# Two-segment ScalarE and VectorE instructions, and a new deal of the PSUM banks, in a two-layer similarity kernel

## The reference

```python
s = box_sum(box_sum(x, 1, 1), 2, 5)               # width sum
num = box_sum(s * s, 3, 20)                       # channel sum
d = box_sum(box_sum(box_sum(x * x, 1, 1), 2, 5), 3, 20)
return jnp.nan_to_num(num / (d * norm), nan=1.0)  # norm: columns inside the window
```

## Time and profile before

| | |
|---|---|
| time, median of 3 runs | 6088.27 us (6087.27 to 6088.81) |
| profiled execution, first to last instruction | 6085.2 us |
| TensorE matmul busy | 5723.6 us, 94% |
| ScalarE busy | 5014.0 us, 82% |
| VectorE busy | 4144.7 us, 68% |
| GpSimd busy | 3546.7 us, 58% |
| mean granted TensorE clock | 0.998 of full speed |
| store of a tile, from issue to landing, median | 18.1 us (18.2 in the first layer) |

### The profile page before, as it was taken

How to read it: one execution, slowest core, us unless ns; L and a number is a source line. 1 busy time by engine, 2 the same in 40 slices (tenths; PEclk the granted TensorE clock), 3 DMA queues, 4 the chain that set the end, 5 groups by cost and what they waited for, 6 DMA issues and landing times.

```text
span 6085.2 us, 139173 instructions
## 1 busy us (share of the span) xinstructions
PE 5723.6 (94%) x49196; PEld 5710.7 (94%) x49196; DVE 4144.7 (68%) x9033; ACT 5014.0 (82%) x8201; POOL 3546.7 (58%) x1043
## 2 busy tenths in 40 slices
PE   0089999999999999999999999999999999999999
PEld 0089999999999999999999999999999999999999
DVE  9988889988877766767667555555555555555555
ACT  0078888888888888888888888888888888888888
POOL 0056665566556666666665666666666666666665
PEclk9999999999999999999999999999999999999999
DMA  9946655556633433434334344343434434343343
GB/s 367 367 157 212 223 207 191 207 203 215 220 125 125 151 138 134 156 124 153 137 135 147 132 147 143 129 160 124 159 130 141 149 124 165 124 153 137 135 154 124
DMA packets 660641, 1007.81 MB, mean 166 GB/s; under 512 B 5168, under 2 KB 660528, under 8 KB 660528
## 3 DMA queue, kind: packets, MB, share of 16 engines
q1 hardware_dynamic: 660528, 1006.65, 47.1%
HBM read 603.98 MB, written 402.65 MB: 165 GB/s over the span
## 4 chain that ended last, share of the span: by engine, by line
PE 89%; DVE 8%; issue 2%; ACT 1%; DMA 0%; SPq 0%; DVEq 0%; POOL 0%; POOLq 0%; ACTq 0%
PE width_ps L468 43%; PE den_ps L492 23%; PE num_ps L492 23%; DVE out_stats L555 3%; DVE lane_mv L562 2%; DVE y_out L649 1%; DVE newton L631 1%; DVE recip L637 0%; DMA y_out<-in_x_dram 0%; DVE beside_stats L555 0%; ACT recip L398 0%; ACT recip L401 0%; SPq L198 0%; DVEq L555 0%; PE num_ps L443 0%
## 5 line engine op out<-in xcount | busy, mean ns | idle before, releaser
L312 POOL TENSOR_TENSOR centred<-x_in,mean_row 128x1536 f32<-128x1536 f32 x512 | 1771.0, 3459 | 1415.0 <-PE width_ps L468 1097.5
L321 POOL TENSOR_TENSOR y_out<-x_in,y_out 128x1536 f32<-128x1536 f32 x512 | 1771.4, 3460 | 1117.1 <-DVE y_out L649 1117.1
L631 DVE SCALAR_TENSOR_TENSOR newton<-den_ps,recip 128x384 f32<-128x384 f32 x2048 | 1110.7, 553 | 1884.7 <-ACT recip L401 1854.8
L492 PE MATMUL den_ps<-band_c,tT 128*128 128x138 f32 (+2 forms) x12288 | 1809.0, 283 | 9.6 <-DVE newton L631 9.6
L492 PE MATMUL num_ps<-band_c,sT 128*128 128x138 f32 (+2 forms) x12288 | 1732.6, 284 | 20.4 <-DVE recip L637 20.1
L468 PE MATMUL width_ps<-band_w,centred 128*128 128x130 f32 x12288 | 1628.3, 275 | 0.5 <-DVE rvar_col L620 0.5
L468 PE MATMUL width_ps<-band_wc,square 128*128 128x130 f32 x12288 | 1625.5, 275 | 0.0
L492 PEld LDWEIGHTS den_ps<-band_c,tT 128*128 128x128 f32 x12288 | 1608.9, 190 | 13.3 <-DVE newton L631 11.8
L492 PEld LDWEIGHTS num_ps<-band_c,sT 128*128 128x128 f32 x12288 | 1580.5, 190 | 27.7 <-DVE recip L637 22.9
L388 ACT ACTIVATE sT<-width_ps,rstd_col 128x512 f32<-128x512 f32 x1536 | 1035.8, 674 | 592.9 <-PE width_ps L468 592.9
L468 PEld LDWEIGHTS width_ps<-band_w,centred 128*128 128x128 f32 x12288 | 1507.0, 191 | 0.9 <-DVE rvar_col L620 0.9
(11 more groups left out here) (44 smaller groups left out, 302.8 us busy)
## 6 DMA issues: line engine op xcount, KB each, us to landing
x_in<-in_x_dram SPq DMA_DIRECT2D x80, 3072.0 KB, 11.0
first_layer_out<-y_out SPq DMA_DIRECT2D x64, 3072.0 KB, 18.2
x_in<-first_layer_out SPq DMA_DIRECT2D x64, 3072.0 KB, 10.9
out_dram<-y_out SPq DMA_DIRECT2D x63, 3072.0 KB, 18.1
beside<-in_x_dram SPq DMA_DIRECT2D x30, 3072.0 KB, 11.0
y_out<-in_x_dram SPq DMA_DIRECT2D x18, 3072.0 KB, 24.4
out_dram<-y_out SPq DMA_DIRECT2D x4, 768.0 KB, 3.5
```

Source lines behind the costliest of these rows:

```text
L312: nc.gpsimd.tensor_tensor(centred[e % 2][:], x_in[slot][:, g * PSEG:(g + 1) * PSEG, :], mean_row[ph % 2][:].unsqueeze(1).to_broadcast([P, ...
L321: nc.gpsimd.tensor_tensor(y_out[slot][:, g * PSEG:(g + 1) * PSEG, :], x_in[slot][:, g * PSEG:(g + 1) * PSEG, :], y_out[slot][:, g * PSEG:( ...
L492: last = nc.tensor.matmul(bank[:, lo:hi], data[:, k, at:at + P], band_c[k][:], start=(k == 0), stop=(k == KB - 1), skip_group_check=True)
L631: nc.vector.scalar_tensor_tensor(newton[:, i, :], den_ps[i % 3][:, 0:C], TINY, recip[par][:, i, :], ALU.add, ALU.mult).then_inc(den_used, 1)
```

## The change

The three parts of the PSUM deal and the widening go together.

- ScalarE: `squares` is one instruction of 1536 instead of two of 768. `invert` works on two segments at once (768 elements out of two banks): 2 Ln and 2 Exp a pair instead of 4 and 4. Its step is S0 T0 L0 S1 T1 Q S2 T2 L1.
- VectorE: `approach` and `weigh` work on two segments at once, 2 and 2 a pair instead of 4 and 4. The result of `approach` goes into `y_out`, where it will be divided in place; the buffer `newton` is gone. The waits for the store of the tile before and for its measurement move from `divide` to the first `approach`. The step is approach 0, weigh 0, approach 1, weigh 1, divide; the three parts of `measure_beside` stand behind approach 0, weigh 0 and approach 1.
- PSUM: `width_ps` is 2 banks, one for S and one for T. `den_ps` is two double banks, D0 and D1 in one, D2 and D3 in the other. `num_ps` is one double bank for N0 and N1 and then for N2 and N3.
- TensorE: N1 is moved ahead of S2 and D2 behind it. The done counts go up once for two segments.
- At a change of phase, the request for the group mean stands behind the last `weigh`, where it was ahead of it.

```diff
-        newton = sb("newton", [P, PSEG, C])
...
-        width_ps = [... for i in range(3)]   # [P, 2 * W]
-        den_ps = [... for i in range(3)]     # [P, 512]
-        num_ps = [... for i in range(2)]     # [P, 512]
+        width_ps = [... for i in range(2)]   # [P, 2 * W]
+        den_ps = [... for i in range(2)]     # [P, 2, 512]
+        num_ps = ...                         # [P, 2, 512]
...
+                    nc.scalar.activation(square[par][:], centred[par][:], ACT.Square).then_inc(rows_squared, 1)
...
-                    src = width_ps[u % 3][:]
+                    src = width_ps[is_t][:]
...
+                    both = recip[par][:, 2 * h:2 * h + 2, :]
+                    nc.scalar.activation(both, den_ps[h][:, :, 0:C], ACT.Ln, bias=bias_ln[:],
+                                         scale=LN_SCALE).then_inc(log_done, 1)
+                    act.wait_ge(log_done, (base + p) * 2 + h + 1)
+                    nc.scalar.activation(both, both, ACT.Exp, bias=bias_exp[:], scale=-1.0).then_inc(recip_done, 1)
...
-                    for what in ("S0", "L0", "T0", "L1", "S1", "Q0", "T1", "L2", "Q1", "S2", "T2", "L3"):
+                    for what in ("S0", "T0", "L0", "S1", "T1", "Q", "S2", "T2", "L1"):
...
-                    if not (is_opening(ph, p, 1) and u < 3):
+                    if not (is_opening(ph, p, 1) and u < 2):
-                        pe.wait_ge(width_taken, (ph * NPAIR + p) * UNITS + u - 2)
+                        pe.wait_ge(width_taken, (ph * NPAIR + p) * UNITS + u - 1)
...
+                        bank, data = num_ps[:, i % 2, :], sT[par]
+                        if i % 2 == 0 and not (is_opening(ph, p, 1) and h == 0):
+                            pe.wait_ge(num_used, pair * 2 + h)
...
+                        bank, data = den_ps[h][:, i % 2, :], tT[par]
+                        if i % 2 == 0 and not is_opening(ph, p, 1):
+                            pe.wait_ge(den_used, pair * 2 + h - 1)
...
-"S0", "F1", "D0", "F2", "T0", "D1", "S1", "F3", "N0", "T1", "D2", "S2", "N1", "T2", "D3", "N2", "N3"
+"S0", "F1", "D0", "F2", "T0", "D1", "S1", "F3", "N0", "T1", "N1", "S2", "D2", "T2", "D3", "N2", "N3"
...
+                    nc.vector.scalar_tensor_tensor(y_out[slot][:, at:at + 2, :], den_ps[h][:, :, 0:C], TINY,
+                                                   recip[par][:, 2 * h:2 * h + 2, :], ALU.add, ALU.mult
+                                                   ).then_inc(den_used, 1)
...
+                            approach(ph, p, par, 0, i, lo, e)
+                            measure_beside(ph, i, lo, e, 0)
                             weigh(ph, p, par, 0)
+                            measure_beside(ph, i, lo, e, 1)
+                            approach(ph, p, par, 1, i, lo, e)
+                            measure_beside(ph, i, lo, e, 2)
                             weigh(ph, p, par, 1)
```

More of the change, by code:

```diff
@@ L360, in finish_logs, with squares @@
                                          scale=-0.5).then_inc(log_given, 1)
[L362 to L370, removed]
+                def squares(ph, p, par):
+                    act.wait_ge(rows_centred, ph * NPAIR + p + 1)
+                    if not is_opening(ph, p, 2):
+                        act.wait_ge(width_done, (ph * NPAIR + p - 1) * UNITS)
+                    nc.scalar.activation(square[par][:], centred[par][:], ACT.Square).then_inc(rows_squared, 1)
                 def take(ph, p, par, k, is_t):
@@ L411, in step @@
                         elif what[0] == "Q":
                             if ph2 < NP_:
-                                squares(ph2, p2, par, n)
+                                squares(ph2, p2, par)
                         elif ph1 < NP_:
-                            take(ph1, p1, 1 - par, n, int(what[0] == "T"))
+                            take(ph1, p1, 1 - par, int(what[1]), int(what[0] == "T"))
                 finish_logs(0)
                 for p in range(2):
-                    for half in range(2):
-                        squares(0, p, p, half)
+                    squares(0, p, p)
@@ L442, in finish_part @@
                         for half in range(2):
-                            last = nc.tensor.matmul(num_ps[part - 1][:, 0:GROUPS], over_p[:],
+                            last = nc.tensor.matmul(num_ps[:, part - 1, 0:GROUPS], over_p[:],
                                                     stat_two[:, 2 * (part - 1), half, :],
@@ L447, in finish_part @@
                         for k in range(KB):
-                            last = nc.tensor.transpose(den_ps[2][:, P * k:P * (k + 1)],
+                            last = nc.tensor.transpose(den_ps[1][:, 0, P * k:P * (k + 1)],
                                                        rstd_row[:, P * k:P * (k + 1)], identity[:])
@@ L623, in finish @@
                     dve.wait_ge(params_ready, ph + 1)
-                def approach(ph, p, par, i):
-                    dve.wait_ge(recip_done, (ph * NPAIR + p) * PSEG + i + 1)
-                    if i == 0 and not is_opening(ph, p, 1):
-                        dve.wait_ge(ratio_done, ph * NPAIR + p)
-                    nc.vector.scalar_tensor_tensor(newton[:, i, :], den_ps[i % 3][:, 0:C], TINY,
-                                                   recip[par][:, i, :], ALU.add, ALU.mult).then_inc(den_used, 1)
```

90 lines of the change are left out of this document (38 added, 52 removed).

## The result

The changed kernel takes 6131.37 us (6131.34 to 6133.99, 4 runs) against 6087.77 (6086.86 to 6088.81, 4 runs) of the kernel before on the same chip: 1.0073 times as long, 95% interval 1.0058 to 1.0087. That is slower, as forecast, but by 43.6 us where 17.4 were forecast, and 1.4 us above the range.

A forecast was written before the change was run, and what follows sets the result against it. TensorE, busy 94% of the span, was taken as the bound, with 56.5 us lost to win. Terms 16 + 2 - 4 + 2.4 + 1 = +17.4 us on 6085.2, plus 3.1 for the median, gave 6106; range 6092 to 6130.

The forecast's parts named there:

- Edit 2: In measured tiles N2 waits for weigh 0 behind a longer chain: 0.59 us a tile, 27 tiles, +16 us.
- Edit 1: ScalarE's fewer, wider instructions: gain nothing; the take of S1 ends 0.5 us before S2 needs its bank.
- Edit 3: Stretches of totals, where VectorE sets the pace: +2 us for three in the first phase, -4 for three later.
- Edits 4: Change of phase: TensorE's first F part waits 1.2 us more for VectorE's request; two outside the totals, +2.4 us.
- 5: The tail: last Ln and Exp 0.6 us longer, `approach` and `weigh` 0.8 between them, some overlapped before: +1 us.
- 6: Waits moved to the first `approach`: stores land well before the next `approach` into their buffer, so nothing.
- A: Rival: the waits of N2 for weigh 0 in measured tiles don't appear; 6090, no change; chance 0.20.
- B: Rival: faster, the chain also fits the stretches of totals and waits for `den_ps` go; -12 us, 6076; chance 0.06.
- C: Rival: wide ScalarE instructions cost two narrow ones, S2 waits in each pair; 6180 to 6230; 0.06 with other cliffs.
- D: Rival: granted clock falls more often after longer or denser waits; +6 us, 6112; counted within the forecast's 0.68.

The follow-up runs named there:

- experiment 1: Changed kernel with the first part of the measuring beside placed behind weigh 0 instead of ahead of it: 6101.92 us, ratio 1.0024.
- experiment 7: Kernel before with two width banks, one for S and one for T, in place of three in turn: 6088.48 us, ratio 1.0001.
- Experiment 2: Changed kernel with two single numerator banks and a narrow `weigh`, four times a pair over one segment: 6119.02 us, ratio 1.0051.
- experiment 3: Changed kernel with a narrow `invert`: Ln and Exp over one segment each, four of each a pair: 6107.22 us, ratio 1.0033.
- experiment 5: Changed kernel with `weigh`, numerator banks, Ln and Exp all narrow; `approach` stays wide over double denominator banks: 6095.67 us, ratio 1.0013.
- number 9: Kernel before with five of its six stretches of totals spread, each set over seven pairs, mostly 4 groups a pair: 6075.82 us, ratio 0.9981.
- 6: Changed kernel with `weigh`, numerator banks, Ln, Exp narrow, first measuring part behind the second `weigh`, mean request ahead of the last: 6092.49 us, ratio 1.0007.
- 4: Changed kernel with the buffer `newton` back and the waits for the store and the measurement back at `divide`: 6126.19 us, ratio 1.0062.

## Why the prediction came out as it did

**Edit 2 was right, in mechanism and in size.** Predicted were 0.23 + 0.10 and 0.16 + 0.10 us in a measured tile, 0.59 together. Measured: steps that are 0.38 and 0.26 us longer than 11.117, 0.64 together, the waits being 0.28 and 0.16. D3 to N2 took 12.12 and 12.38 us where the sum said 12.07 (4 groups) and 12.33. The order of the terms held too: with the first part of the measuring moved, experiment 1, the loss is nil.

**Edit 1 was right.** The stated cover of 0.5 us holds for all 510 pairs; no wait of a width unit for a take appears, with the wide Ln and Exp or, in experiment 7, without them. In a late pair the take of S1 ends at 5549.77 and S2 starts at 5550.35, a cover of 0.58. I took 0.30 us more for 384 more elements. Measured are 901 - 578 = 323 ns for Ln and 936 ns less the 0.61 us of the earlier trace rows for Exp: 0.84 and 0.85 ns an element. That agrees with the 0.833 of the Trainium skill (ScalarE: Activation LUTs, What happens when an `exp` ACTIVATE runs) better than with my 0.77.

**Edit 3 is the step that failed.** For a later stretch the prediction put "three more pairs cost 3 x 0.87 + 0.98 + 1.67 + 2.09 + 3.8 - 11.12 = 0.0 to 0.1 and a restart each: 2.8 against 4.1". It added up VectorE's work and took it for the period, as if VectorE never waited while it is the slowest. It does wait, about 1 us in each pair of the first later stretch: 0.93 for N2 and N3 in the first turn, since one double bank serves both of its `weigh`, and 1.14, 0.93 and 1.14 for ScalarE's Exp in the others. The prediction charged the chain from D3 to N2 once a stretch, where every D3 that is on time starts it anew. So the last three pairs there lost 1.12, 1.33 and 1.12 us where it had 0.0 to 0.1 and a restart, and N2 waited four times a stretch and not once. Measured are 6.0, 7.7 and 7.7 us, together 13 us more than forecast; 9.7 of these are the mechanism and 3.3 the clock. Experiment 2 took the exchange away, 3 shortened the chain, 5 did both, and these gave back 0.8, 0.6 and 1.5 us of the 1.9 that a stretch costs more than before, with the clock left out. In the first phase the stretches cost 7 us more than the +2 forecast; how those divide between chain, exchange and the clock (below) no run here separates, but experiment 5 gives 6.2 us back there and experiment 1, with less in the chain, 7.8.

**Terms that weren't in the sum at all:** 5.1 us at the starts of loop bodies and 1.1 in the first body, where 16 groups stand behind a `divide` in place of 8. **Edits 4, 5 and 6** came out at 2.0 for 2.4, 1.4 for 1, and no wait for a store. As forecast, TensorE loses nothing more once the last change of phase (3361 to 3373 us) is over.

**The rivals.** A (no waits) fell: they are there, at the predicted place. B (faster, as the waits ahead of the denominators go) had half of its mechanism: those waits are gone, but the totals made the numerators late instead. The rule of the Trainium skill on few large instructions (VectorE: DVE Perf Modes, The TRN2 errata) agrees in direction with VectorE's row: 2048 instructions fewer took 167 us off its busy time, 0.08 us each. The kernel became slower all the same. C (twice the price) fell with 936 ns where it needed 1220. D (the clock) came true, and may have cost more than its +6: the mean granted clock went from 0.998 to 0.997, and while pairs run it falls nine times where it fell four times before. Each fall takes 1.7 us of full-speed time, so up to 8.5 of the 44.4 us are its part, 3.3 of them in the later stretches.

## What to carry to other kernels

Widening an instruction also doubles what its buffer holds up. Before counting the saved instructions, write down who fills the bank and who empties it: with one bank the two engines' times can add, as they did in experiment 3. Then follow a late unit through two turns: a unit that stands ahead of it in the order is on time and starts the same chain again. In both cases the busy sum of the slower engine is not the period. Where an engine is idle for a third of the time, its rare dense stretches set the price, and spreading those (11.5 us gained, with not one instruction changed in kind) was worth more here than making each instruction cheaper. And a wait too short for the list of waits can still be read from the distance between unit starts.

## What the runs showed of the hardware that was not expected

**The clock behind some waits.** TensorE's timeline of the kernel after in the first stretch of totals, where the earlier trace rows were before:

```profile
977.63 2.47 PE L486 MATMUL num_ps<-band_c,sT 128*128 128x138 f32 x12 [3.92 <-DVE recip L638]
...
993.91 1.70 PE L486 MATMUL num_ps<-band_c,sT 128*128 128x138 f32 x12 [3.23 <-DVE recip L638]
...
1009.19 3.18 PE L486 MATMUL num_ps<-band_c,sT 128*128 128x138 f32 x12 [3.90 <-DVE recip L638]
```

The same unit in the second and third of the later stretches:

```profile
2568.82 3.02 PE L486 MATMUL num_ps<-band_c,sT 128*128 128x138 f32 x12 [2.19 <-DVE recip L638]
...
3287.99 2.03 PE L486 MATMUL num_ps<-band_c,sT 128*128 128x138 f32 x12 [2.19 <-DVE recip L638]
```

And the granted clock in stretches of 1 us, around the first row and behind 2568.82: the stretch, its length, busy time of PE, PEld, DVE, ACT and POOL with counts, PEclk, DMA share, GB/s:

```profile
977.00:978.00 1.00, 0.37 (x3) 0.37 (x4) 1.00 (x3) 0.00 (x0) 0.00 (x0) 1.00 1.07 378
978.00:979.00 1.00, 1.00 (x9) 1.00 (x8) 1.00 (x3) 0.00 (x0) 0.00 (x0) 0.71 1.05 370
979.00:980.00 1.00, 1.00 (x6) 1.00 (x6) 1.00 (x5) 0.00 (x0) 0.00 (x0) 0.50 1.05 370
...
2570.00:2571.00 1.00, 1.00 (x6) 1.00 (x6) 0.00 (x0) 0.00 (x0) 0.00 (x0) 0.50 1.06 402
```

After two waits of 3.9 us the same twelve records take 2.47 and 3.18 us instead of 1.70: the clock is at its lower level of 1.2 GHz, 0.50 in the rows, for some 3 us. After 3.23 us of waiting it isn't. A wait of 2.19 us ahead of N2 was enough at 2568.82 and 3287.99 and not at 1846.76, with the same work around it; in experiment 2 it was so with 2.10 us (2.49 us at 2556.36, 1.70 at 2582.62). The two later stretches with a fall cost 7.7 us and the one without 6.0, so a late bank can cost 1.7 us on top of its wait. What decides is not shown. Runs with the same waits can therefore differ by some microseconds: summed over every microsecond in which pairs run, what the granted clock falls short of full speed is 6.8 us in the kernel before, 15.4 in the kernel after, 13.7 in experiment 1, 20.5 in 2, 13.6 in 3, 15.3 in 5 and 5.1 in 9.

**VectorE at the start of a loop body.** Its timeline in the kernel after, at one of the four starts:

```profile
1356.75 2.17 DVE L550 BATCH_NORM_STATS2 out_stats<-y_out 128x192 f32 x8
1359.39 0.96 DVE L630 SCALAR_TENSOR_TENSOR y_out<-den_ps,recip 128x768 f32<-128x768 f32 x1 [0.47 <-DVE out_stats L550]
1361.56 0.88 DVE L550 BATCH_NORM_STATS2 beside_stats<-beside 128x192 f32 x3 [1.21 <-issue]
```

Behind the first `approach` VectorE executes nothing for 1.21 us, and waits for nothing that the profile shows. Four such gaps cost TensorE 5.1 us here, because the chain of edit 2 has no slack. They aren't tied to one line: number 9, in the old arrangement, has them too, up to 1.6 us ahead of `approach` (8 times, 6.7 us) and up to 1.1 ahead of the measuring (4 times, 4.0 us). Experiments 2 and 6 have none behind `approach` but 0.7 to 1.0 us ahead of it, experiment 1 has shorter ones (1.9 us in 4), and experiments 3 and 4 have none, though 3 keeps the moved waits and 4 doesn't. So the moved waits don't decide it. Something at the back jump that depends on the program's layout would fit, but no run here shows the cause. It stays open.
